# A graph kernel whose GpSimd scatters in the adjacency stage no longer wait for a mark that TensorE sets per batch

## The reference, cut to what matters

```python
# layer 0: five steps of a normalised neighbourhood sum (ALPHA = 0.8)
def step(h, _):
    m = jax.ops.segment_sum(w[:, None] * h[row], col, num_segments=n)   # w = dinv[row] * dinv[col]
    h = (1.0 - ALPHA) * m + ALPHA * x
    return (h, None)
...
x = _layernorm(x + _L0_gnn_ref(x, edge_index), axis=-1)
# layer 1: a gate per edge from a small network on edge_attr (200000 x 40), then a sum per source node
gate = jax.nn.silu(edge_attr @ W1.T + b1) @ W2.T + b2
...
msg = gate * h[dst] * (cw * mj)[:, None]
agg = jax.ops.segment_sum(msg, src, num_segments=N)
...
```

## Time and profile before

| | |
|---|---|
| Median of 3 runs | 4071.46 us (4066.48 to 4079.98) |
| Profiled execution | 4073.36 us, span 4071.6 us |
| Adjacency stage | 119 to 1408 us |
| Busy shares of the span | TensorE matmul 67%, VectorE 67%, GpSimd 58%, ScalarE 34% |
| Scatters (L710), both stages | 1568, 1780.0 us busy, 1135 ns each |

### The profile page before, as it was taken

How to read it: one execution, slowest core, us unless ns; L and a number is a source line. 1 busy time by engine, 2 the same in 40 slices (tenths; PEclk the granted TensorE clock), 3 DMA queues, 4 the chain that set the end, 5 groups by cost and what they waited for, 6 DMA issues and landing times. The chain is left out here.

```text
span 4071.6 us, 105324 instructions
## 1 busy us (share of the span) xinstructions
PE 2725.1 (67%) x35364; PEld 2318.9 (57%) x35364; DVE 2732.0 (67%) x5976; ACT 1370.2 (34%) x4059; POOL 2374.3 (58%) x2008
## 2 busy tenths in 40 slices
PE   1565555656566378777777877777837777777772
PEld 1343334434344267666666767666727777777772
DVE  6876667666767464454554454454579999999997
ACT  1533333333333211011111111111126666666662
POOL 3267777777777646555555555555545555555552
PEclk9755555555555599888998888888868888888886
DMA  7433333333342288777888878778746666666663
GB/s 268 160 143 143 143 143 128 143 143 142 142 107 93 86 317 297 280 286 276 289 295 284 298 278 287 275 285 294 250 151 226 225 225 225 227 224 229 232 225 92
DMA packets 228303, 870.94 MB, mean 214 GB/s; under 512 B 89444, under 2 KB 148708, under 8 KB 183075
## 3 DMA queue, kind: packets, MB, share of 16 engines
q1 hardware_dynamic: 167130, 728.90, 50.5%
q10 hardware_dynamic: 9768, 96.89, 6.1%
q0 software_dynamic: 51232, 42.56, 3.4%
HBM read 670.80 MB, written 197.52 MB: 213 GB/s over the span
## 5 line engine op out<-in xcount | busy, mean ns | idle before, releaser
L710 POOL DMA_INDIRECT slot_table<-w_pay,w_slot x1568 | 1780.0, 1135 | 1120.1 <-PEq L1222 494.3
L1224 PE MATMUL pL<-p_parts,p_adj 128*128 128x144 bf16 x12250 | 979.4, 241 | 354.7 <-issue 249.2
L1224 PEld LDWEIGHTS pL<-p_parts,p_adj 128*128 128x128 bf16 x12250 | 885.4, 105 | 445.0 <-issue 439.6
L1036 PE MATMUL pA<-ohk,ohb 128*128 128x98 bf16 x3200 | 361.6, 276 | 508.2 <-ACT adj L1072 264.3
L1036 PEld LDWEIGHTS pA<-ohk,ohb 128*128 128x128 bf16 x3200 | 258.4, 132 | 640.6 <-ACT adj L1072 329.6
L1600 ACT ACTIVATE h_all<-c_rows,c_ac 128x48 f32<-128x48 f32 x2401 | 561.2, 323 | 81.2 <-DVE c_ac L1569 81.2
L1072 ACT ACTIVATE adj<-pA 128x392 bf16<-128x392 f32 x800 | 368.2, 494 | 514.0 <-PE pA L1036 255.1
L1476 POOL TENSOR_TENSOR c_msg<-c_msg 128x637 f32<-128x637 f32 x196 | 233.0, 1189 | 443.9 <-DVE c_msg L1538 443.9
L797 ACT ACTIVATE w_hid<-w_pH,b1c 96x512 f32<-96x512 f32 x196 | 133.9, 683 | 908.5 <-remote 436.5
L1675 PE MATMUL cG<-c_tabp,c_ohT 128*128 128x81 bf16 x7056 | 380.0, 225 | 4.5 <-issue 2.7
L1675 PEld LDWEIGHTS cG<-c_tabp,c_ohT 128*128 128x128 bf16 x7056 | 356.0, 115 | 6.2 <-issue 3.5
(11 more groups left out here) (277 smaller groups left out, 3260.5 us busy)
## 6 DMA issues: line engine op xcount, KB each, us to landing
p_adj<-adj_table SPq DMA_DIRECT2D x250, 1568.0 KB
c_lanes<-lane_table SPq DMA_DIRECT2D x150, 768.0 KB, 6.6
adj_table<-adj ACTq DMA_DIRECT2D x50, 1568.0 KB
c_rows<-slot_table SPq DMA_DIRECT2D x255, 255.0 KB, 4.3
slot_table<-zero SPq DMA_DIRECT2D x42, 1249.5 KB
c_lanes<-lane_table SPq DMA_DIRECT2D x50, 832.0 KB
w_attr<-in_edge_attr_dram SPq DMA_DIRECT2D x49, 640.0 KB
slot_table<-w_pay,w_slot POOLq DMA_INDIRECT x1568
```

What stands on the lines that cost most here:

```text
L710: pool.indirect_dma_start(slotT, bass.IndirectOffsetOnAxis(ap=slot[:, t:t + 1], axis=0), pay[:, t, :], None, bounds_check=SLOTS - 1, oob_i ...
L1036: m = nc.tensor.matmul(pA[:, n % 2, j * KG:(j + 1) * KG], ohb[:, b % OB, g * (PT // 2) + j, :], ohk[:, b % OB, g * (PT // 2) + j, :])
L1224: x_ = nc.tensor.matmul(pL[:, half, o * H3:(o + 1) * H3], adj[:, q, n * P:(n + 1) * P], parts[:, n, :, :].rearrange("p t f -> p (t f)"), s ...
```

## The change

GpSimd's two functions that wait for a mark (`in_step`, `in_single`) go, in the adjacency alone; with them go the semaphores `a_turn` and `a_poolgo`, and TensorE's increments. The same marks in the propagation (`p_turn`) stay. The scatters still wait for their rows, for the cleared table and, before a buffer is freed, for earlier scatters to land.

```diff
-                s_clear, s_turn, s_poolgo = sem("a_clear"), sem("a_turn"), sem("a_poolgo")
+                s_clear = sem("a_clear")
...
                         with pool.Fori(0, DOUBLE) as w:
                             pool.wait_ge(s_clear, w + 1)
-
-                            def in_step(t):
-
-                                pool.wait_ge(s_turn, w * (2 * MARKS) + (18 + t * (2 * MARKS - 8) // WT))
-                                pool.sem_inc(s_poolgo, 1)
-                            win.scatter(pool, w, in_step)
+                            win.scatter(pool, w)
                         with pool.Fori(DOUBLE, W0) as w:
                             pool.wait_ge(s_clear, w + 1)
-
-                            def in_single(t):
-
-                                pool.wait_ge(s_turn, w * MARKS + (DOUBLE * MARKS + 10 + t * MARKS // WT))
-                                pool.sem_inc(s_poolgo, 1)
-                            win.scatter(pool, w, in_single)
+                            win.scatter(pool, w)
...
                         def batch(D, b):
                             pe.wait_ge(s_oh, D * NBAT + b + 1)
-                            pe.sem_inc(s_turn, 1)
...
-                        pe.sem_inc(s_turn, 2 * MARKS)
```

## The result

The changed kernel takes 4253.05 us (median of 4 runs, 4241.94 to 4288.05), the kernel before 4074.52 us beside it. The ratio is 1.045, 95% interval 1.042 to 1.048: 178 us slower. The forecast was slower, 4130 us, with a range of 4005 to 4185; the sign was right and the size was not.

A forecast was written before the change was run, and what follows sets the result against it. The adjacency stage was taken as bound by TensorE's and ScalarE's loop of groups and copies, handed over late while scatters run and are queued. From the profiled 4073.4 us, +69 and -10 gave 4132, set to 4130; range 4005 to 4185.

The forecast's parts named there:

- (e): First window of the adjacency stage, 164 to 217 us: paced by its rows as much as by marks; 0.
- (c): Adjacency windows, what GpSimd's stands covered: one TensorE group a stand turns slow, 46 stands at 1.5 us; +69 us.
- (d): End of the adjacency stage, GpSimd alone after TensorE's last group: it loses a stand and most of its lag; -10 us.
- (f): Propagation: it keeps its marks, and no leftover scatter can run into it; 0.
- (a): TensorE's 400 increments beside its waits: no array instruction moved, sequencer runs ahead; 0, bounds 0 to 20 us.
- (b): GpSimd's stands in the adjacency stage: they go, idle time moves ahead of a window's first rows; by itself saves nothing.
- The loop doesn't care: TensorE's group loop: quick stretches had reasons of their own, leaving only the stage end's gain, 4061 us, or nothing; chance 0.16.
- GpSimd drained at the right moment: Adjacency windows: GpSimd dry at the first rows shortens each window; at most 4006 us, more likely 4010 to 4050; chance 0.30.

The follow-up runs named there:

- e4: Changed kernel with TensorE's 400 increments put back and no wait of GpSimd on them; 4274.26 us, ratio 1.045 to the kernel before.
- e13: The changed kernel itself run once more; 4266.4 us, ratio 1.044 to the kernel before.
- e3: Changed kernel without the 768 scatters of the adjacency stage; 3810.64 us, ratio 0.934 to the kernel before.
- e9: Changed kernel with GpSimd stopped after every four scatters until its engine's write is done; 3691.01 us, ratio 1.023, beside a kernel before of 3609 us.
- e18: Changed kernel with GpSimd stopped after 16 of a window's 32 scatters and ahead of the first; 3623.61 us beside 3601.84 for the kernel before, 1.006.
- e15: Changed kernel with a GpSimd write after every two scatters, waiting only for the write before the last two, so without a pause; 4309.43 us, ratio 1.046.
- e17: Changed kernel with GpSimd stopped after every eight scatters until its engine's write is done; 4095.38 us beside 4110 for the kernel before, 0.995.
- e12: Changed kernel with GpSimd stopped after every four scatters until its engine's write is done; 4075.13 us beside 4084 for the kernel before, 0.998.
- e16: Changed kernel with a GpSimd write ahead of every fourth scatter, waited for behind it, so one to five stay queued; 4274.71 us, ratio 1.037.
- e1: Changed kernel, each adjacency scatter waiting until the scatter two before it has landed; 4393.67 us, ratio 1.076 to the kernel before.
- e11: Kernel before with each mark two turns of TensorE later; 3615.17 us beside 3609 for the kernel before, 1.001.
- e14: Kernel before with each mark two turns of TensorE later, run again; 4154.26 us beside 4084 for the kernel before, 1.016.

## Why the prediction was right in sign and wrong in size

The profiled execution of after is 214.5 us longer in its span. Its parts, from the starts of the first rows (L899) of windows 1 and 23 and of the next stage's first ScalarE instruction:

| part | before | changed | difference | predicted |
|---|---|---|---|---|
| to the first rows of window 1 | 216.3 | 228.6 | +12.3 | (e) 0 |
| windows 1 to 23 | 1139.5 | 1342.4 | +202.9 | (c) +69 |
| first rows of window 23 to the next stage | 61.1 | 54.0 | -7.1 | (d) -10 |
| rest of the span | 2654.7 | 2661.1 | +6.4 | (f) 0 |

**(a), the increments: 0.** Right; e4 is the test.

**(b), the stands: right in kind.** The first scatter now goes 1.8 us behind the first rows (mean of windows 1 to 22), and the idle time lies ahead of it. It is 15 us, not the 5 to 9 I wrote, since the window is 61 us and not 52 to 56.

**(c) is the step that failed, as a size.** "I take one group a stand", each 1.5 us slower than a quick one, 3 us a window. Measured: 9.1 us a window in this execution and 7.8 in e13's, made up of 15.1 us more in turns 12 to 1 and 6 less elsewhere. Both factors were off. The copies of turns 12 and 13 stand not 2.04 but 6.1 us apart on average (1.6 before). And it wasn't one group a stand: in each window some five groups, of turns 12 to 14, are over 3 us late (106 in 22 windows). What came back elsewhere, 5.0 us in turns 9 to 11, was put at nothing. I had worked out the upper bound, three groups a stand or +207 us, which with (d) comes to 4270, and then left it outside the range. (The range's upper end is a slip besides: two groups a stand are 138 us, which with (d) gives 4199, not 4185; the measured time lies above both.) It was left out on the ground that every window would get a quick time of its own when GpSimd restarts. It does, and I had misplaced it: the hand-overs of the first 5 us behind a window's first scatter take 0.8 us on average, but those issued 5 to 10, 10 to 15 and 15 to 20 us behind it 4.2, 12.3 and 14.4 us. The first rows come when TensorE is at turn 8 to 10, mostly 8, so the quick time falls on turns 9 to 11, where 15 us less lateness gave back 5.0 us, and the slow one on turns 12 to 14, where late hand-overs cost most. The thought that a late hand-over beside the network costs little stood in the prediction; applied to where the lateness would go, and not only to where the idle time would go, it would have led to the upper bound.

**The cause behind (c).** The prediction said "while scatters are running and queued" and left the mechanism open. The running part is shown as a condition, though not as a sufficient one: without scatters no hand-over is late (e3), but in the sets of e9 and e18 scatters run and none is late either. The queued part is refuted (e15). A pause of GpSimd's engine does count: 0.88 us after every eight scatters removes the change's cost (e17), after every four nearly all lateness too (e12), and that the marks worked through the pauses they made is the reading that fits. e15 and e16 have writes of the same kind, so the write itself isn't what helps. The pauses also hold GpSimd back: in e12 its first scatter goes 11 us behind the first rows, in e15 2.0 us. That difference doesn't look like the cause, since in e17 the windows in which it was under 4 us have no more lateness than the others (49 and 56 us), but no run separates the two.

What makes the signal of a finished group late stays open. It isn't a matter of how many scatters are under way (1.9 in e12, 1.5 in the changed kernel) or of busy DMA engines (7 to 9% above). Whether late signals come out together with landings can't be told: 21% lie within 0.1 us of a recorded landing, 12% if shifted by 0.3 us, of 94, but the trace of the changed kernel holds only 2,620 of the 12,288 updates that the landings of the stage's 768 scatters make at 16 each. The gaps in the record go with the lateness themselves: e15 has 2,483 of them, the kernel before 4,326, e12 5,925, e1 9,918, and e11, without late hand-overs, 12,067. Whether signals and records are held up by the same thing, and whether the writing of the records has a part in it, no run shows. An unbroken run isn't enough by itself: hand-overs issued 30 us and more behind a window's first scatter are prompt again (0.4 to 1.5 us) while GpSimd runs on for some 15 us; those turns have the network's work on TensorE. Whether one pause in the middle of 32 scatters would do was to be told by e18, which fell in the wrong set.

**Where the condition is another, so is the change.** With prompt hand-overs, GpSimd alone is the bound: windows of 48.3 us in e11, where 32 scatters of 1.21 us with 0.30 us between them fill 48.2, and 49.0 in e18. The changed kernel itself was not timed there. What differed in those sets is in part visible. e14 and e11 are one kernel, and their spans are 4157.5 and 3615.3 us; only 156 us of that lie ahead of the propagation, and 391 in it. The stretch from 1700 to 2500 us (columns as above), e14 first:

```profile
1700.00:2500.00 800.00, 615.61 (x7026) 542.34 (x7024) 403.29 (x1184) 94.85 (x138) 452.39 (x412) 0.89 0.79 283
1700.00:2500.00 800.00, 711.88 (x9518) 664.46 (x9515) 548.04 (x1590) 127.92 (x188) 624.06 (x561) 0.96 0.96 374
```

The same loads came at 283 GB/s in one and 374 in the other. So a slower way to memory goes together with the late hand-overs. e3, without a scatter in the adjacency stage, has the slow loads too (284 GB/s in its propagation) and no late hand-over. A rival stands untested, then: that GpSimd's scatters hold TensorE's signals up only while something outside the kernel holds up the memory.

**(d), the end: -7 us** of -10, and close by luck. From the first rows of window 23 to TensorE's last matmul it takes 14.3 us longer (38.0 in place of 23.7), which is (c) again, and from there to the next stage 21.3 us less (16.1 in place of 37.4), twice what was forecast. The last scatter comes at 1613.18 us, 4 us behind TensorE's last group, against 27 before. It doesn't end the stage any more: the last two copies come 15 and 9 us behind their groups, at 1615.85 and 1617.99 us, and the block's store after them.

```profile
1613.18 0.98 POOL L710 DMA_INDIRECT slot_table<-w_pay,w_slot  x1 [0.31 <-issue]
...
1625.03 1.28 ACT L1231 ACT_TABLE_LOAD   x1 [6.54 <-PEq L91]
```

**(e) and (f), both taken as 0**, came to +12 (13 in e13) and +6 us. The first window was called paced by its rows as much as by marks; it was 12 us more.

**The rivals.** "The loop doesn't care" had the rule of the Trainium skill, "SBUF — State Buffer", section "Who interferes with whom", behind it, by which (c) would be 0: 4061 us forecast, 4253 measured. That doesn't show the rule wrong of the SBUF's ports: e12 and e15 move the same bytes with the same engines, and only one of them is slow, which speaks against a port as what holds TensorE's groups back, though no run looks at a port. "GpSimd drained at the right moment" would have needed first and last rows under 12 us apart; they are (9 to 12 us in nearly every window), and the windows got longer all the same. That sign, which I had named as proof of the rival, proves nothing: the rows come together because the hand-overs of turns 9 to 11, beside the network, are prompt now (5.2 us of lateness in place of 20.5).

## What to carry to other kernels

An engine that "only waits" may be what lets its neighbours through: before a throttle is taken out, look at what the neighbours do while the throttled engine stands, and price its removal with what they do in the places that the work moves to. When a bound has been worked out from rows and only a softer argument speaks against it, the bound belongs in the range. And a throttle needs to be neither frequent nor tied to another engine: one short pause of GpSimd after eight scatters did what 32 waits on TensorE's marks did, 0.995 of their time where hand-overs are late and 1.017 where they are prompt, so it is no clear gain over them.

## What the runs showed of the hardware

- Beside an unbroken run of GpSimd's indirect transfers ScalarE stood up to 13.5 us for a group that TensorE, otherwise idle, had long issued, and the recorded update of the group's semaphore was as late; without them a group is handed over in some 0.3 us.
- It does so under one condition of the machine and not under another: the kernel before took 4074 to 4110 us in five comparisons and 3602 and 3609 us in two, and two chips were met in both. In the first the propagation's loads ran at 283 GB/s (e14), in the second at 374 (e11). What makes the condition is not known.
- A write of 128 words by GpSimd between two scatters, waited for by its own sequencer, costs 0.7 us; waited for only two scatters later it costs nothing (1.29 us from scatter to scatter in e15, 1.28 without).
- A wait for the landing of the scatter two before takes GpSimd from 1.28 to 2.05 us a scatter (65.7 us in 32), with single stands of up to 5.8 us.
